# A three-layer conditioned transformer on one core: where VectorE makes the second batch's moments and root at the end of the second layer's MLP

## What is computed

```
m0..m5 = split(silu(c) @ ada_w + ada_b, 6)
y = modulate(layer_norm(x), m0, m1)
x = x + m2 * attention(y)            # 16 heads of 18 channels
y = modulate(layer_norm(x), m3, m4)
x = x + m5 * (gelu(y @ w1 + b1) @ w2 + b2)   # 288 -> 1152 -> 288
```

## Time and profile before

| | |
|---|---|
| time, median of 3 runs | 1544.54 us |
| lowest and highest run | 1533.57 and 1544.72 us |
| the profiled execution, whole | 1555.99 us |
| its span, first to last instruction | 1554.3 us |
| mean granted TensorE clock | 0.970 |
| busy: TensorE, VectorE, ScalarE, GpSimd | 92%, 78%, 60%, 46% |

### The profile page before, as it was taken

One profiled execution on the slowest core, in us unless ns is written; L12 is line 12 of the kernel. 1 busy time (PEld: TensorE's weight loads), 2 busy tenths in 40 slices (PEclk: granted clock), 3 DMA queues, 4 the chain that ended last, 5 costly groups with the idle time before them and its releaser, 6 DMA issues.

```text
span 1554.3 us, 26773 instructions
## 1 busy us (share of the span) xinstructions
PE 1436.2 (92%) x8963; PEld 977.9 (63%) x8963; DVE 1218.5 (78%) x2469; ACT 931.6 (60%) x1687; POOL 720.3 (46%) x1620
## 2 busy tenths in 40 slices
PE   7899999888999998994999998888999999989998
PEld 5653334767899887873633335887875333478885
DVE  7789996896987587665889998577877999866643
ACT  4458887555666554664378877333744888754432
POOL 0656650115666343045666667667765566640000
PEclk9999999999999999996999999999998999999999
DMA  8765530129654644335735422111165453000001
GB/s 204 226 179 121 146 84 3 38 86 269 170 142 118 189 128 133 103 118 149 228 88 150 121 53 37 16 6 19 5 203 173 119 142 97 5 3 1 1 1 61
DMA packets 108245, 160.70 MB, mean 103 GB/s; under 512 B 33860, under 2 KB 75830, under 8 KB 107976
## 3 DMA queue, kind: packets, MB, share of 16 engines
q1 hardware_dynamic: 101964, 142.85, 30.8%
q0 software_dynamic: 6144, 16.14, 8.4%
HBM read 114.74 MB, written 39.58 MB: 99 GB/s over the span
## 4 chain that ended last, share of the span: by engine, by line
PE 53%; DVE 16%; ACT 4%; issue 3%; DMA 2%; another core or an unknown queue 1%; SPq 1%; POOL 1%; DVEq 0%; ACTq 0%; POOLq 0%
PE psum L1641 17%; PE psum L1831 8%; PE psum L1820 6%; PE psum L1794 6%; PE psum L2122 5%; PE psum L2265 5%; PE psum L1704 1%; DVE bn L2475 1%; DVE x_norm L2503 1%; DVE hid_lo L3224 1%; DMA raw_a<-in_L_cond_b 1%; DVE hid_lo L3067 1%; PE psum L2405 1%; PE psum L1970 1%
## 5 line engine op out<-in xcount | busy, mean ns | idle before, releaser
L1560 ACT ACTIVATE probs<-psum 128x512 f32<-128x512 f32 x768 | 401.9, 600 | 87.7 <-PE psum L1820 87.2
L2663 DVE TENSOR_REDUCE minus_max<-psum 128x1 fp32r<-128x512 f32 x450 | 288.7, 683 | 30.2 <-PE psum L1794 28.8
L1641 PE MATMUL psum<-x_split,w_hi 128*128 128x512 f32 (+1 forms) x684 | 244.3, 400 | 12.1 <-DVE x_tail L2521 5.0
L1794 PE MATMUL psum<-k_stack,q_stack 54*128 54x512 f32 x768 | 246.5, 456 | 8.7 <-DVE minus_max L2663 2.7
L1820 PE MATMUL psum<-q_stack,k_stack 55*128 55x512 f32 x768 | 244.3, 452 | 0.7 <-ACT probs L1560 0.4
L1831 PE MATMUL psum<-probs,o_t 128*19 128x512 f32 x1536 | 205.9, 608 | 6.1 <-ACT o_t L1539 3.2
L1092 POOL TENSOR_TENSOR qr_m<-qr_m 64x8 f32<-64x8 f32 (+35 forms) x544 | 191.1, 351 | 42.6
L2658 DVE TENSOR_REDUCE minus_max<-psum 128x2 fp32r<-128x1024 f32 x159 | 193.9, 1220 | 20.6 <-PE psum L1794 20.5
L1820 PEld LDWEIGHTS psum<-q_stack,k_stack 55*128 55x128 f32 x768 | 119.3, 188 | 127.2 <-ACT probs L1560 115.4
L1794 PEld LDWEIGHTS psum<-k_stack,q_stack 54*128 54x128 f32 x768 | 116.5, 188 | 129.2 <-DVE minus_max L2663 61.9
L1087 POOL TENSOR_TENSOR qr_m<-qr_rows 64x288 f32<-64x288 f32 (+31 forms) x64 | 45.2, 707 | 252.3 <-DMA qr_rows<-qr_rows 252.3
(11 more groups left out here) (450 smaller groups left out, 3238.2 us busy)
## 6 DMA issues: line engine op xcount, KB each, us to landing
qk_parts_d<-qk_parts SPq DMA_DIRECT2D x48, 512.0 KB
raw_b<-in_L_cond_w SPq DMA_DIRECT2D x36, 432.0 KB
q_stack<-qk_parts_d SPq DMA_DIRECT2D x96, 144.0 KB
k_stack<-qk_parts_d SPq DMA_DIRECT2D x96, 144.0 KB
raw_a<-in_L_cond_w SPq DMA_DIRECT2D x36, 384.0 KB
q_stack<-qk_parts_d SPq DMA_DIRECT2D x96, 72.0 KB
k_stack<-qk_parts_d SPq DMA_DIRECT2D x96, 72.0 KB
moe_out_d<-branch SPq DMA_DIRECT2D x9, 576.0 KB, 3.4
```

Of the source, the lines that this page charges most:

```text
L1560: act.activation(PE_[:, v // 4, 2 * hf + pr, :], psum[:, score_bank(16 * i + v), :], ACT.Exp, scale=SCALE).then_inc(s_e, 1)
L1641: i = pe.matmul(dst, a, r, start=(n == 0), stop=(n == len(terms) - 1))
L1794: return pe.matmul(psum[:, bank, :], Q6[half(hf, STK), g, pr, P * qt:P * qt + P], K6[half(hf, STK), g, pr, :], start=True, stop=True)
L2663: dve.tensor_reduce(MX[:, i % 2, col:col + 1], psum[:, bank, :], AX.X, ALU.max, negate=True).then_inc(s_mx, 1)
```

## The change

`ffn_sum` no longer makes the moments and the root of the second batch (b = 1); it still does for the first and the third. The moments are made one unit later, at u = 25, behind `low` of the fourth batch and `normalise` of the first batch, and the root at u = 26, behind `hidden_parts` of that unit. `normalise` of the second batch at u = 27 reads both, as before.

```diff
@@ -3248,7 +3248,7 @@
                 dve.wait_ge(s_xr, NT * f + TT * (b + 1))
-                if f == sets_of(l)[-1] and l + 1 < LAYERS and b < B - 1:
+                if f == sets_of(l)[-1] and l + 1 < LAYERS and b in (0, 2):
                     stats(b)
@@ -3426,11 +3426,15 @@
                     if l + 1 < LAYERS and j >= J - UNITS:
+                        if u == NEXT_UNIT[1] - 1:
+                            rsqrt(1)
                         for b, first in enumerate(NEXT_UNIT):
                             if u == first:
                                 normalise(l + 1, 0, b)
                             if u == first + 3:
                                 low(l + 1, 0, b)
+                        if u == NEXT_UNIT[1] - 2:
+                            moments(1)
```

## The result

| | before | changed |
|---|---|---|
| median of 20 runs each | 1541.3 us | 1537.93 us |
| lowest and highest | 1533.57 and 1545.71 | 1533.96 and 1543.33 |
| span of the profiled execution | 1554.3 us | 1535.1 us |

The ratio is 0.9972, with a 95% interval from 0.996 to 0.9984: 4.3 us faster (2.5 to 6.2), less than 1%. The 19 us between the two profiled spans are not the change's. The fourth batch's transposes (L1704), which lie ahead of every moved instruction, start at 1072.34 in one and at 1056.84 in the other, so 15.5 us of it had come about before.

A forecast was written before the change was run, and what follows sets the result against it. The prediction took VectorE to bound this place, TensorE being busy 1436.2 of 1554.3 us. A gain of 5.3 us, the middle of leads of 5.1 and 5.4, off the median 1544.54 gave 1539.2 us, range 1530 to 1546.

The forecast's parts named there:

- The wait for x_tail goes whole, with 0.6 us to spare: Before unit 27, the fourth batch's first matmuls: TensorE's 4.0 us wait for VectorE vanishes, x_tail done 0.6 us early.
- The new pause of 1.3 us for the evacuation: At unit 27's second-weight group (L2265): TensorE waits some 1.3 us for the third batch's first evacuation.
- VectorE 5.1 us earlier at hid_lo of 28: VectorE's queue after the moved work: hid_lo of 28 starts at 1089.6 instead of 1094.75, with the root taken as 3.07.
- The slow stretch, 2.67 us: Unit 27's matmuls and the twelve behind: 1.73 + 0.94 us lost at 1.2 GHz after the pause, to be saved.
- The lead survives: From hid_lo of 28 through the last layer's projections and attention: both engines keep a lead of 5.1 to 5.4 us.
- Rival 1: At the new pause before unit 27's second-weight group TensorE's clock falls, costing about 2.67: gain 2.6, 1541.9; chance 0.10.
- Rival 2: Order indifferent: hid_lo of 26 and 27 come late, the wait only changes its name; gain below 1, 1544; chance 0.06.
- Rivals 3 and 4: Last attention's start: low-clock stretch longer (3: slower, 1546, chance 0.08) or shorter or gone (4: 1535.4 to 1532.4, chance 0.16).

The follow-up runs named there:

- the second profile of the new order: The changed kernel with the sums of the last 6 of 64 reflectors of GpSimd's QR left out: ratio 0.9964 to the kernel before.
- two more profiles of the same code in this stage: The kernel before with GpSimd's last 6 QR reflectors without their sums, ratio 1.0013, or with one product made four times more in them, 0.9998.
- QR early: The kernel before, or the changed one, with the sums of the last 6 of 64 reflectors of GpSimd's QR left out: ratios 1.0013 and 0.9964.
- QR late: The kernel before with one product made four times more in the last 6 reflectors of GpSimd's QR: ratio 0.9998.
- normalise behind the evacuation: The changed kernel with normalise of the second batch moved from unit 27 to 28, behind the third batch's evacuation: ratio 0.999 to the kernel before.
- filled pause: The kernel before with 17 more matmuls of 512 columns on TensorE in front of its wait for the fourth batch's low parts: ratio 1.0007.
- the root twice in the old place: The kernel before with the second batch's root made twice where it stood: ratio 1.0034.
- root twice in the new place: The changed kernel with the second batch's root made twice at unit 26: ratio 1.0023 to the kernel before.
- Going on from the change: Three kernels from the changed one: second batch's normalise behind the evacuation, 0.999; third batch's moments and root moved too, 0.9991; second batch's moments and root left out, 0.9983.

## Why the prediction was right

The forecast was 5.3 us faster, 1539.2; measured were 4.3, and a median of 1537.93. That the two medians lie only 1.3 us apart has some luck in it: the forecast started from 1544.54, the median of three runs, and the median of twenty is 1541.3, from which 5.3 us less would be 1536.0. Point by point:

- **The wait for x_tail goes whole, with 0.6 us to spare.** Nearly: 0.16 was left and there was nothing to spare. VectorE's new idle before hid_lo of 25 was 1.30 us, not 0.4: the branch products and hid_lo of 24 ran 0.8 us faster this time (the products 1.56 against 1.97), so VectorE stood waiting for hid_hi sooner. It got it when forecast (4.79 us after the transposes, forecast 4.74), but what followed ran slower (1.04 and 1.64 for 0.69 and 1.22), and that used up the 0.6.
- **The new pause of 1.3 us for the evacuation.** Measured 1.24 and, in the second profile of the new order, 1.18.
- **VectorE 5.1 us earlier at hid_lo of 28.** Measured 4.62 (22.41 - 17.79). The root took 2.44, not the 3.07 that I took; the slower instructions above (0.8 together) and hid_lo of 26 (1.11 to the next start, for 0.7) more than ate it.
- **The slow stretch, 2.67 us.** This is the term that was mis-sized. It was right for the one profile that I had; two more profiles of the same code in this stage lost 1.7 and 1.4 us to it. With the QR early, the groups of the earlier trace rows read 3.35 and 1.67, for 3.35 and 2.53. The stage's gain is 4.7 us by the first profile and 2.8 by the other two. Of the 1.9 between these, the clock is 1.0 to 1.3; the later waits for hid_lo make most of the rest (1.7 in the first, 0.8 in each of the other two). The chain of the kernel before with the QR early:

```profile
1067.23 3.35 PE psum L1641 x7
1070.58 1.67 PE psum L2265 x12
```

- **The lead survives.** To the first score matmul it is 77.6 to 78.8 before and 72.8 to 73.7 changed, 4.8 in the mean. Between projection and scores the three profiles differ by 2.7 us, so the two ends of the stage aren't equally good measures. Behind it the changed kernel had 1.0 us less lead at its end than at the projection, which one profile can't tell from chance.
- **Rival 1** (the new pause costs the clock) didn't happen in either profile of the new order, but at 4.62 and, in another order, at 1.91 us it does: its mechanism is real and the change stands near it. **Rival 2** is refuted by the waits. **Rivals 3 and 4** can't be told apart from the spread. At the start of the last attention the lower clock takes 6.8 us in the kernel before (a granted clock of 0.66 from 1185 to 1205) and 5.2 in the changed one (0.74 from 1165 to 1185), but 3.4 in the kernel before with the QR late (0.83 from 1170 to 1190) and 6.8 in the changed one with normalise behind the evacuation (0.66 from 1178 to 1198). And from the first score matmul to the last layer's MLP the profiles take 220.7 to 224.1 us, in either direction for old and new order alike.

## What to carry to other kernels

In a pipe whose engines have nearly equal loads, the place of a side job is judged by how late it makes the next delivery that TensorE waits for, not by its sum: 5 us in front of the urgent piece cost a pause of 4 us and a slow stretch, the same work behind it, in one piece or in two (or the root alone), left pauses of 1.2 to 1.7 and no slow stretch. Before the same move is made at the next place, add up what already stands between the two deliveries there; with 3.3 us of weight parts in that gap it made things worse. A slow stretch read from one profile is one draw: in seven profiles it cost from 1.4 to 2.8 us, and behind the longest pause, 5.81 us, only 1.5.

## What the hardware showed beside

- The clock behind pauses of about the same length isn't the same each time. In the stage and just ahead of it, it stayed at 1.00 behind pauses of 1.67, 1.89 and 1.92 us and fell behind one of 1.91. Some 40 us ahead of the stage, at the third batch's transposes, it stayed at 1.00 behind pauses of 2.4 us in four kernels (filled pause, normalise behind evacuation, and the two before with the QR early or late), and in the one with the root twice in the old place it fell behind one of 1.29. In the last MLP it fell behind 2.03 to 2.04 in three of five, behind 2.40 to 2.75 in six of seven, not behind the one of 3.21. In the stage it fell at every pause of 3.87 and more. So no length between 1.3 and 3.2 us decides it alone.
- Instructions of VectorE can take longer while GpSimd works: the 128x512 hid_lo takes 0.69 us and never over 0.71 where no GpSimd instruction overlaps it, and up to 1.30 where one does (1.19 in the changed kernel's stage); instructions of four columns take 0.16 and up to 0.68 in the stage, L2491 with one input among them. The Trainium skill, page "SBUF — State Buffer", section "Who interferes with whom", says that VectorE contends with a GpSimd instruction that reads SBUF in instructions with two inputs in SBUF; the pause that follows the QR's end agrees. It exempts an instruction with one such input outside VectorE's 2-port modes; whether L2491 runs in one of these no run here shows.
- The chip on which the last four kernels ran (root twice in the new place, and those of "Going on from the change") was slower as a whole: there the kernel before had a median of 1556.65 us instead of 1540 to 1541. Only the ratios compare.
